# Attention sums divided in the layout of o's weights after a pass through DRAM, and x added by TensorE in the tail

## The reference

```python
def proj(W):
    return (in_features @ W.T).reshape(B, S, H, d_k).transpose(0, 2, 1, 3)
scores = jnp.einsum('bhqd,bhkd->bhqk', Q, K) / math.sqrt(d_k)
scores = jnp.where(causal, -jnp.inf, scores)
attn = jax.nn.softmax(scores, axis=-1)
out = jnp.einsum('bhqk,bhkd->bhqd', attn, V)
return out.transpose(0, 2, 1, 3).reshape(B, S, D) @ o_proj.T
...
x = x + _L0_attn_ref(_layernorm(x, axis=-1), ...)
x = x + _L0_ffn_ref(_layernorm(x, axis=-1), ...)
```

## Time and profile before

| | us |
|---|---|
| median of 3 runs | 393.17 |
| lowest, highest | 392.19, 395.23 |
| the profiled execution | 393.18 |
| its span on the core | 391.4 |
| PE busy (matmuls) | 354.2 |
| ACT busy | 279.5 |
| DVE busy | 209.7 |
| POOL busy | 47.8 |

### The profile page before, as it was taken

The page is one execution under the profiler, slowest core; times in us unless marked ns, Lnnn a source line. Parts: engine busy times, 40 slices in busy tenths (PEclk is TensorE's granted clock), DMA queues, the critical chain, the costliest instruction groups (busy, mean ns, idle before and its releaser), DMA issues.

```text
span 391.4 us, 6977 instructions
## 1 busy us (share of the span) xinstructions
PE 354.2 (90%) x2558; PEld 138.0 (35%) x2558; DVE 209.7 (54%) x711; ACT 279.5 (71%) x317; POOL 47.8 (12%) x75
## 2 busy tenths in 40 slices
PE   8967978899998999999999999998999899799874
PEld 3545524354333444423323233232322323222542
DVE  4555558455755654555447464546346543600785
ACT  2544438677887877888788887888878688799311
POOL 5011000000011100011121111211112111100040
PEclk9997969999999999999999999999999999999997
DMA  6479444222450022271000000000000000000001
GB/s 202 139 224 315 116 131 141 55 55 54 124 148 13 2 54 75 62 214 44 13 2 13 3 13 16 3 13 2 13 16 0 16 0 15 13 2 3 0 3 55
DMA packets 29380, 23.31 MB, mean 60 GB/s; under 512 B 15392, under 2 KB 25888, under 8 KB 29344
## 3 DMA queue, kind: packets, MB, share of 16 engines
q1 hardware_dynamic: 29344, 22.84, 19.8%
HBM read 12.35 MB, written 10.49 MB: 58 GB/s over the span
## 4 chain that ended last, share of the span: by engine, by line
PE 63%; DVE 20%; ACT 7%; issue 6%; POOL 2%; DMA 1%; DVEq 0%; ACTq 0%
PE acc L713 23%; PE scores L696 12%; PE aux L596 7%; ACT probs L814 6%; PE aux L651 5%; PE aux L637 3%; DVE probs L1010 2%; PE aux L662 2%; PE aux L602 2%; PE aux L623 1%; DVE ffn L1055 1%; POOL exp_gap L1216 1%; PE aux L644 1%; DVE gates L1083 1%; DVE parts L954 1%
## 5 line engine op out<-in xcount | busy, mean ns | idle before, releaser
L814 ACT ACTIVATE probs<-scores 128x1024 f32<-128x1024 f32 x272 | 260.2, 1032 | 69.1 <-PE scores L696 59.1
L713 PE MATMUL acc<-probs,v_aug 128*32 128x512 f32 (+3 forms) x1280 | 145.4, 545 | 1.3 <-ACT probs L814 0.9
L696 PE MATMUL scores<-q_stack,k_stack 64*128 64x512 f16 (+3 forms) x640 | 86.5, 352 | 3.7 <-ACT probs L814 2.0
L696 PEld LDWEIGHTS scores<-q_stack,k_stack 64*128 64x128 f16 x640 | 21.1, 94 | 103.6 <-ACT probs L814 80.3
L1010 DVE TENSOR_TENSOR probs<-probs,mask_sb 128x512 f32<-128x512 f32 (+1 forms) x80 | 44.2, 577 | 22.5 <-ACT probs L814 22.0
L713 PEld LDWEIGHTS acc<-probs,v_aug 128*32 128x32 f32 x1280 | 30.8, 110 | 49.8 <-issue 29.7
L596 PE MATMUL aux<-xT,wqkv_sb 128*128 128x128 f32 x192 | 26.3, 294 | 1.0 <-DVE xT L941 1.0
L596 PEld LDWEIGHTS aux<-xT,wqkv_sb 128*128 128x128 f32 x192 | 24.0, 203 | 5.4 <-issue 3.1
L952 DVE CAST parts<-qk 128x512 f16<-128x512 f32 x12 | 5.1, 427 | 36.5 <-ACT qk L806 36.5
L1207 POOL TENSOR_TENSOR rstd<-ve,minus_half 128x1 f32<-128x1 f32 x12 | 7.3, 608 | 101.6 <-DVE ve L932 101.6
L1211 POOL TENSOR_TENSOR rstd<-ve,minus_half 128x1 f32<-128x1 f32 x12 | 6.6, 549 | 103.8 <-DVE ve L1040 103.8
(11 more groups left out here) (146 smaller groups left out, 323.0 us busy)
## 6 DMA issues: line engine op xcount, KB each, us to landing
q_stack<-q_dram SPq DMA_DIRECT2D x32, 128.0 KB, 2.8
k_stack<-k_dram SPq DMA_DIRECT2D x32, 128.0 KB, 2.8
qk_dram<-qk SPq DMA_DIRECT2D x12, 256.0 KB, 2.5
x_sb<-x SPq DMA_DIRECT2D x3, 512.0 KB, 6.4
q_dram<-parts SPq DMA_DIRECT2D x12, 128.0 KB, 2.0
...
out<-result SPq DMA_DIRECT2D x12, 128.0 KB, 1.7
...
```

Of the source, the lines that this page charges most:

```text
L696: m = pe.matmul(scores[u % BANKS][:, j, col:col + n], k_stack[row:row + STACK, kb // TPC, 2 * i + p, kb % TPC * P:(kb % TPC + 1) * P], q_s ...
L713: m = pe.matmul(acc[32 * hp:32 * hp + 32, lo:CHUNK], v_aug[:, kb, QUAD * i + hp, :], probs[:, u % PROBS, hp % 2, col:col + CHUNK - lo], st ...
L814: act.activation(probs[:, u % PROBS], scores[u % BANKS][:], ACT.Exp, scale=EXP_SCALE).then_inc(exp_done, 1)
```

## The change

- **Sums through DRAM.** sums has one buffer now. When the two quads of a half m (m = 0, 1) of a chunk are finished, SP stores their 128 x 2 x 512 sums to sums_dram (store_sums, one step later) and loads them back (load_sums, three steps later, four DMAs of 64 rows of 2 KB) in another order of rows: attn[.., m, 0] has 128 numerators (q, d, head) by 512 tokens, attn[.., m, 1] the denominator of each. That is seven (c, m) pairs: the last, (3, 1), stays as before.
- **Division there.** divide(c, m, t) on DVE: reciprocal of 128x128 in place, product of 128x128, for each of the four tiles t of a chunk. Division t stands at step s + 7 + t, s being the step of the pair's last group. The steps: 13 to 16, 18 to 21 (chunk 0), 31 to 34, 44 to 47 (chunk 1), 65 to 68, 86 to 89 (chunk 2), 115 to 118 (first half of chunk 3).
- **o reads the result directly.** wo's rows are put into the same order on the host (attn_order). The pieces turn_sums and turn_back and their DVE work are gone from tiles 0 to 11. A tile may start after DIVIDED_STEP of its chunk (21, 47, 89).
- **Tail.** In step 137, ahead of the last groups, PE computes for each of the four tiles x by the identity and the first half of o into the tile's bank (residual). Behind the last sums only the second half is transposed (two transposes a tile), divided (divide_last), transposed back (one) and multiplied. y then is the bank itself: ACT copies it (keep_y), DVE's addition is gone.
- SP's loop runs over 138 steps instead of 136.

```diff
-SUMS_STEP = [max(s for s, ns in GROUPS_AT.items() if any(GROUPS[n].c == c for n in ns)) for c in range(NCHUNK)]
+
+
+DIVIDE_LAG = 7
+SUMS_AT = {}
+for _s, _ns in GROUPS_AT.items():
+    for _n in _ns:
+        if GROUPS[_n].last and GROUPS[_n].i % 2 == 1 and (GROUPS[_n].c, GROUPS[_n].i) != (NCHUNK - 1, NQUAD - 1):
+            SUMS_AT.setdefault(_s, []).append((GROUPS[_n].c, GROUPS[_n].i // 2))
+
+
+def steps_of_divisions():
+    at = {}
+    for s, pairs in SUMS_AT.items():
+        for c, m in pairs:
+            for t in range(TPC):
+                at.setdefault(s + DIVIDE_LAG + t, []).append((c, m, t))
+    return at
+
+
+DIVIDE_AT = steps_of_divisions()
+DIVIDED_STEP = [max(s for s, ds in DIVIDE_AT.items() if any(d[0] == c for d in ds)) for c in range(NCHUNK)]
...
-POST_PIECES = ("turn_sums", "turn_back", "o", "turn_y", "ffn", "turn_gated", "lora")
-POST_GAP = {"turn_sums": 1, "turn_back": 1, "o": 2, "turn_y": 1, "ffn": 2, "turn_gated": 1, "lora": 1}
+POST_PIECES = ("o", "turn_y", "ffn", "turn_gated", "lora")
+POST_GAP = {"o": 2, "turn_y": 1, "ffn": 2, "turn_gated": 1, "lora": 1}
...
-                if len(flying) < 2 and post_next < TILES - TPC and s > SUMS_STEP[post_next // TPC]:
+                if len(flying) < 2 and post_next < TILES - TPC and s > DIVIDED_STEP[post_next // TPC]:
...
-TAIL_STAGES = {"turn_sums": -2, "turn_back": 0.5, "o": 1.5, "normalise": 3, "turn_y": 4,
+TAIL_STAGES = {"residual": -9, "turn_sums": -2, "turn_back": 0.5, "o": 1.5, "normalise": 3, "turn_y": 4,
...
-        sums = sb("sums", [P, 3, NQUAD, CHUNK])
+
+
+        held = sb("held", [P, NQUAD + 4 * KH, CHUNK])
+        sums = held[:, 0:NQUAD]
+        attn = held[:, NQUAD:NQUAD + 4 * KH].rearrange("p (c m n) t -> p c m n t", m=KH, n=2)
...
-        tail_banks = [scores[0][:, 0], scores[0][:, 1], scores[1][:, 0], scores[1][:, 1]]
-        tail_turn_banks = [scores[2][:, 0, 0:P], scores[2][:, 1, 0:P], aux[:, 0:P], acc[:, 0:P]]
+        tail_units = [len(UNITS) - BANKS + t // 2 for t in range(TPC)]
+        tail_banks = [scores[u % BANKS][:, t % 2] for t, u in enumerate(tail_units)]
+        last_scores = scores[(len(UNITS) - 1) % BANKS]
+        tail_turn_banks = [last_scores[:, 0], last_scores[:, 1], aux[:], acc[:]]
...
+        def attn_of(n, m):
+            if isinstance(n, int):
+                if (n // TPC, m) == (NCHUNK - 1, KH - 1):
+                    return buffers(n).attn_t
+                return attn[:, n // TPC % 2, m, 0, n % TPC * P:(n % TPC + 1) * P]
+            return gen_attn_t[:, m, :]
+
+
+        def divided_upto(c, m, t):
+            return (KH * c + m) * TPC + t + 1
...
+            def store_sums(c, m):
+                sp.wait_ge(acc_read, NQUAD * c + 2 * m + 2)
+                sp.dma_start(sums_dram[c, m], sums[:, 2 * m:2 * m + 2, :]).then_inc(sums_out[m], 16)
+
+            def load_sums(c, m):
+                sp.wait_ge(sums_out[m], 16 * (c + 1))
+                if c >= 2:
+                    sp.wait_ge(o_psum, TPC * (c - 1))
+                rows = sums_dram[c, m].rearrange("(h n d) q t -> n q d h t", h=QUAD, n=2)
+                for n in range(2):
+                    for q in range(2):
+                        sp.dma_start(attn[q * P // 2:(q + 1) * P // 2, c % 2, m, n], rows[n, q]).then_inc(sums_in[m], 16)
...
-            for s in range(QK_STEPS):
+            for s in range(STEPS):
...
+                    if slot == 0:
+                        for c, m in SUMS_AT.get(s - 3, ()):
+                            load_sums(c, m)
+                        for c, m in SUMS_AT.get(s - 1, ()):
+                            store_sums(c, m)
...
-            def turn_sums(g):
-                w = buffers(g)
-                pe.wait_ge(acc_read, NQUAD * (g // TPC + 1))
-                for q in range(NQUAD):
-                    t = pe.transpose(w.bank[:, q * P:(q + 1) * P], sums_of_tile(g, q), ident_sb[:])
-                t.then_inc(turned_psum, 1)
-
+
+            def residual(n, w):
+                pe.wait_ge(exp_done, tail_units[n % TPC] + 1)
+                pe.matmul(w.bank[:, 0:D], ident_sb[:], x_sb[:, n, :], start=True, stop=False)
+                pe.wait_ge(divided, divided_upto(NCHUNK - 1, 0, n % TPC))
+                pe.matmul(w.bank[:, 0:D], attn_of(n, 0), wo_sb[:, 0, :], start=False, stop=False)
+
+
+            def turn_sums(n, w):
+                pe.wait_ge(acc_read, NQUAD * NCHUNK)
+                t = n % TPC
+                for q in range(2):
+                    m = pe.transpose(w.sums_bank[:, q * P:(q + 1) * P], sums[:, 2 + q, t * P:(t + 1) * P], ident_sb[:])
+                m.then_inc(turned_psum, 1)
 
             def turn_back(n, w):
-                pe.wait_ge(attn_y_ready, n + 1)
-                for k in range(KH):
-                    t = pe.transpose(w.bank[:, k * P:(k + 1) * P],
-                                     w.attn_y.rearrange("p h d -> p (h d)")[:, k * P:(k + 1) * P], ident_sb[:])
-                t.then_inc(attn_t_psum, 1)
+                t = n % TPC
+                pe.wait_ge(attn_y_ready, t + 1)
+                pe.transpose(w.sums_bank[:, 2 * P:3 * P], w.attn_y, ident_sb[:]).then_inc(attn_t_psum, 1)
 
             def o_proj(n, w):
-                pe.wait_ge(attn_t_ready, n + 1)
-                for k in range(KH):
-                    m = pe.matmul(w.bank[:, 0:D], w.attn_t[:, k, :], wo_sb[:, k, :],
+                if w.in_tail:
+                    pe.wait_ge(attn_t_ready, n % TPC + 1)
+                elif isinstance(n, int):
+                    pe.wait_ge(divided, divided_upto(n // TPC, KH - 1, n % TPC))
+                else:
+                    pe.wait_ge(attn_t_ready, n - TILES + TPC + 1)
+                for k in range(1 if w.in_tail else 0, KH):
+                    m = pe.matmul(w.bank[:, 0:D], attn_of(n, k), wo_sb[:, k, :],
                                   start=(k == 0), stop=(k == KH - 1))
...
+                if s == STEPS - 1:
+                    for t in range(TPC):
+                        run_piece("residual", TILES - TPC + t)
...
+            def keep_y(g):
+                act.wait_ge(o_psum, g + 1)
+                act.copy(buffers(g).y, buffers(g).bank[:, 0:D]).then_inc(y_kept, 1)
...
+            def store_attn_t(g):
+                act.wait_ge(attn_t_psum, g % TPC + 1)
+                act.copy(buffers(g).attn_t, buffers(g).sums_bank[:, 2 * P:3 * P]).then_inc(attn_t_ready, 1)
...
-                dve.tensor_copy(sums[:, c % 3, i, :], acc[:]).then_inc(acc_read, 1)
-
-            def divide(n, w):
-                turned = w.bank.rearrange("p (h d) -> p h d", d=32)
-                dve.wait_ge(turned_psum, n + 1)
-                dve.reciprocal(w.inverse.unsqueeze(2), turned[:, :, DK:DK + 1]).then_inc(inverse_ready, 1)
-                dve.wait_ge(inverse_ready, n + 1)
-                dve.tensor_tensor(w.attn_y, turned[:, :, 0:DK], w.inverse.unsqueeze(2).to_broadcast([P, H, DK]),
-                                  ALU.mult).then_inc(attn_y_ready, 1)
-
-            def store_attn_t(n, w):
-                dve.wait_ge(attn_t_psum, n + 1)
-                dve.tensor_copy(w.attn_t.rearrange("p k t -> p (k t)"), w.bank[:, 0:D]
-                                ).then_inc(attn_t_ready, 1)
+                if c:
+                    dve.wait_ge(sums_out[i // 2], 16 * c)
+                dve.tensor_copy(sums[:, i, :], acc[:]).then_inc(acc_read, 1)
+
+            def divide(c, m, t):
+                n = divided_upto(c, m, t)
+                num, den = (attn[:, c % 2, m, n, t * P:(t + 1) * P] for n in range(2))
+                if t == 0:
+                    dve.wait_ge(sums_in[m], 64 * (c + 1))
+                dve.reciprocal(den, den).then_inc(inverse_ready, 1)
+                dve.wait_ge(inverse_ready, n)
+                dve.tensor_tensor(num, num, den, ALU.mult).then_inc(divided, 1)
+
+            def divide_last(n, w):
+                t = n % TPC
+                turned = w.sums_bank[:, 0:2 * P].rearrange("p (q h d) -> p q h d", q=2, d=32)
+                inverse = w.inverse.rearrange("p (q h) -> p q h", q=2).unsqueeze(3)
+                dve.wait_ge(turned_psum, t + 1)
+                dve.reciprocal(inverse, turned[:, :, :, DK:DK + 1]).then_inc(inverse_ready, 1)
+                dve.wait_ge(inverse_ready, divided_upto(NCHUNK - 1, KH - 1, t))
+                for q in range(2):
+                    m = dve.tensor_tensor(w.attn_y.rearrange("p (q d h) -> p q h d", q=2, h=QUAD)[:, q],
+                                          turned[:, q, :, 0:DK], inverse[:, q].to_broadcast([P, QUAD, DK]), ALU.mult)
+                m.then_inc(attn_y_ready, 1)
 
             def residual_and_stats(n, w, x_tile):
-                base = STATS2 * n
-                dve.wait_ge(o_psum, n + 1)
-                dve.tensor_tensor(w.y, w.bank[:, 0:D], x_tile, ALU.add).then_inc(stats2, 1)
+                base = stats2_before(n)
+                if w.in_tail:
+                    dve.wait_ge(y_kept, n % TPC + 1)
+                else:
```

(23 more changed lines are left out.)

58 lines of the change are left out of this document (33 added, 25 removed).

## The result

The changed kernel takes 403.7 us (median of 4 runs, 402.67 to 404.35) against 393.4 of the kernel before in the same comparison: a ratio of 1.0255, 95% interval 1.0209 to 1.0302. The forecast was 397.7, range 391 to 402. The direction was right, but the time lies above the range. The profiled execution took 403.45, its span is 401.7; against the profiled one of before (393.18) that is 10.3 us more where the sum said 4.5.

A forecast was written before the change was run, and what follows sets the result against it. PE was taken to bound the kernel (busy 90% of the span), ACT as a second floor. 393.2 less 5.8 gained up to the tail, plus 8.3 for divisions and 2.0 in the tail, gave 397.7 us; range 391 to 402.

The forecast's parts named there:

- the steps without a piece: Steps 24 to 123: 24 new ones cost ACT's 1.84 us instead of 1.53, so 7.5 comes back.
- The stops ahead of turn_gated: PE's idle time there over twelve tiles, laid out tile by tile: 8.4 us, against 9.6 before.
- The divisions in steps 10 to 24: Eight divisions in steps 13 to 21 delay v_aug, xT and norms on DVE, costing PE 4.3 us.
- The tail: From step 137: residual matmuls put 3.84 us on the path, 1.8 is gained behind them, so 2.0 longer.
- Rival 2: DVE's slack takes in every division, so the kernel gets faster, 389.4 us; chance 0.08.
- Rival 4: The loads of sums land late and DVE holds PE up twice, 400.9 us; chance 0.06.
- The size of a division: On DVE, a reciprocal of 128x128 at 0.875 us and a product at 0.29: 1.16 in all.
- Rivals 1: Cheap reciprocals on DVE, 0.29 us each: 392.8 us, no change; chance 0.22.
- rival 3: A reciprocal takes eight ordinary columns per column, 1.22 us for 128x128: 401.4 us; chance 0.14.
- the 8.3 of the sum: PE's loss in us from 20 divisions standing in DVE's queue ahead of work that PE wants.
- those of 31 to 34: Divisions ahead of tile 1's gates, 1.1 us, and ahead of yT, 0.2.
- The stops at turn_gated change too: With o (1.06 us) mostly between ffn and turn_gated, the stop there falls to 0.05 if no masks are between.

The follow-up runs named there:

- e1: The changed kernel with each of the 28 divisions cut to one column of 128, same places and waits: 399.07 us, ratio 1.0107.
- e2: The changed kernel with 20 of the 28 whole divisions moved to steps where DVE had been idle: 398.19 us, ratio 1.0086.
- e4: The changed kernel with x added by DVE in the tail again and the four identity matmul pairs gone: 404.25 us, ratio 1.0236.
- e3: The changed kernel with DVE's copy gatedT ahead of normalise and the masks where o precedes turn_gated: 402.14 us, ratio 1.0162.
- e5: The changed kernel with the edits of e2 and e3 together: 392.64 us, ratio 0.9955.
- e8: The changed kernel with one tile at a time, divisions in the steps of e2, three steps instead of two between ffn and turn_gated: 382.18 us, ratio 0.9709.

## Why the prediction was wrong, point by point

**Held.** The twelve tiles' turn_sums and turn_back leave PE, and the steps without a piece run at ACT's pace: 79 to 90 takes 19.5. The stops ahead of turn_gated: 8.4 forecast, 8.9 measured. But the 8.4 was without the divisions, which had terms of their own at tiles 1 and 5; without them it is 7.6 (e1) or 7.2 (e2), and the nearness is in part luck: tiles 3, 5 and 11 came out 2.3 lower together, tile 8 at 1.2 instead of 0.

The divisions in steps 10 to 24: 4.3 forecast, 4.5 measured, and by v_aug, xT and norms as named (groups L651, L659, L671). Steps 44 to 47: 1.0 and 0.9.

The tail: 2.0 forecast; 3.65 for the residuals (I had 4.24, from eight halves of o at 0.53, while successive ones begin 0.43 apart), less the 0.40 of idle time, and from the end of the last values 24.6 against 26.1 before, so 1.5 gained and not 1.8: together 1.75. The stage shows 2.8, because 1.1 of ACT's pace is paid in steps 124 and 125. Inside the 1.5 the terms were wrong: e4 prices DVE's missing additions at 0.4, where I had 1.2 and the gap of 0.26, so the rest of the shorter way (half the transposes, half of o) gave 1.1, where I had 0.3.

Rival 2 is out for the change as it stands, since steps 10 to 24 lost 4.5, though e2 shows that the slack is there when the divisions stand in it. Rival 4 is out: the loads land in 2.7, and DVE waits for them only where nothing follows.

**The size of a division** was near: 0.944 for the reciprocal where the sum took 0.875, 0.319 for the product where it took 0.29, so 1.26 and not 1.16. Rivals 1 (0.29) and 3 (1.22) are out. The slope is 6.2 ns a column (0.155 at one column in e1, 0.944 at 128), six times the 1.04 of the products. The Trainium skill's page "VectorE: DVE Perf Modes", section "Walkthrough: the 8-slice pipeline in each mode", gives Reciprocal a repeat count of 8. Taken as the time of eight ordinary columns, as rival 3 took it, that is not what these rows show.

The divisions as a whole came out cheaper than the 8.3 of the sum: against e1 by stages 4.1, 0.2, 0.9 and, once the 1.7 of one half clock stretch more in e1 is taken off, 1.4, together 6.6. The steps that come out smallest are those of 31 to 34 (1.3 forecast, 0.2 against e1). But the one-column divisions of e1 cost DVE about 0.3 each themselves, and its stop at step 33 is still 2.05. Against e2, which has no division there, these steps cost 0.8 and the half clock's 1.7. All the divisions together, against e2, cost 7.9 from step 10 to the tail, 6.2 of it without the clock.

**The step that failed** is the one that says "The stops at turn_gated change too". It puts "o" between ffn and turn_gated, counts its 1.06 as time that PE passes, and looks for what DVE has ahead of turn_gated. It does name the copy gatedT, but only as delayed by masks, in the 8.4 and in the 1.2 of steps 65 to 68. What DVE gets from that same "o" (y, statistics, aggregate, a wait of 0.67 for POOL, normalise 0.81) stands ahead of gatedT, and lora, one step later, waits for it: 6.7. I had moved PE's instruction and not the DVE instructions that come with it. e3 (stops 6.7 to 0.8, stages -5.6) and e5 (7.1 in e2 to 0.0) show it. The same oversight gives the 1.8 ahead of ffn, where yT stands behind another tile's chain; no run takes it away alone, and e3 and e5 keep it.

**What was not in the sum at all** is the clock. The stops of steps 33 and 58 (2.6 and 2.0) were followed by 3.4 us at a granted 0.50. In a stretch where PE is the bound that costs 1.7 each, so 3.4. The length of a stop alone would not have priced it: the 2.3 of step 68 was not followed by it, nor the same 1.97 at step 58 in e2. The sum took every microsecond of stop for one microsecond of time.

**The sum again.** From step 10 to the tail the change was to cost 8.3 - 5.8 = 2.5; it cost 8.8. The tail cost 2.8 for 2.0, the start and steps 0 to 10, of which nothing was forecast, -1.2 (half clock again: stretches of 6.8 at 34.1 and 51.2 before, of 3.4 at 22.0 and 52.7 after). That is the 10.3 for the 4.5. The 6.3 missing between step 10 and the tail are made up of lora's stops 6.7, ffn's 1.8, half clock 3.4 and turn_gated's stops 0.5, less the divisions' 1.7 and 2.1 for the 24 steps at ACT's pace (42.1 in all, 1.75 each and not 1.84): 8.6. It is 2.3 too much. e3 accounts for most of that: of the stops ahead of lora 1.8 only stand in for stops ahead of the masks and of turn_y, which come when the copy is moved. The rest was not separated.

**What stays open.** Why the half clock follows a stop in one execution and not the same stop in another, and why that of the first 60 us and of the tail differs between executions that do the same. And the kernel before was not tried in the order of e8. Its tiles have seven pieces each where the changed kernel's have five, 84 and 60 in all, so that the freed steps are what e8 spends on the wider gap; that part of e8's gain is therefore the change's own is argued, not shown.
